# A transformer block on one core: the work ahead of the first projection in another order

## What is computed

```python
def _L0_attn_ref(x, Wqkv, bqkv, Wo, bo):           # 16 heads of 32
    kqv = x @ Wqkv + bqkv
    q, k, v = ...
    scores = einsum('bsnh,btnh->bnst', k, q) / sqrt(32)      # causal mask
    attn = softmax(scores, axis=2)
    return einsum('bnkq,bknh->bqnh', attn, v).reshape(b, s, 512) @ Wo + bo

def _L0_ffn_ref(h, gate_w, gate_scale, up_w, up_scale, down_w, down_scale):
    g, u = h @ Wg.T, h @ Wu.T                      # weights (int - 128) * scale
    return (silu(g) * u) @ Wd.T

x = x + _layernorm(_L0_attn_ref(_layernorm(x), ...))
x = x + _layernorm(_L0_ffn_ref(_layernorm(x), ...))
```

## Time and profile before

| | |
|---|---|
| median of 3 runs | 1654.09 us (1651.8 to 1659.24) |
| the profiled execution | 1659.15 us, its span 1657.3 us |
| PE busy over the span | 1552.0 us (94%) |
| DVE, ACT, POOL busy | 941.8, 775.8, 644.8 us |
| mean granted clock of PE | 0.975 |
| first transpose on PE | starts at 10.13 us |
| first projection on PE | starts at 30.95 us |
| first maximum (`mjob 0 0`) on PE | starts at 40.92 us |

### The profile page before, as it was taken

The page is one execution under the profiler, slowest core; times in us unless marked ns, Lnnn a source line. Parts: engine busy times, 40 slices in busy tenths (PEclk is TensorE's granted clock), DMA queues, the critical chain, the costliest instruction groups (busy, mean ns, idle before and its releaser), DMA issues.

```text
span 1657.3 us, 24457 instructions
## 1 busy us (share of the span) xinstructions
PE 1552.0 (94%) x9288; PEld 641.0 (39%) x9288; DVE 941.8 (57%) x1897; ACT 775.8 (47%) x1252; POOL 644.8 (39%) x844
## 2 busy tenths in 40 slices
PE   4899899988999899999897899999999999999997
PEld 2334234323333333343332244444444444444443
DVE  5657665778656777766777333464434343434344
ACT  5356566557566666755775643233222222222222
POOL 4336675677666677757766520020000000000001
PEclk8899999999999999999998999999999999999999
DMA  4222232213411233321354531221111111111000
GB/s 178 90 52 53 56 73 52 58 53 102 113 49 39 78 90 84 95 54 39 116 159 127 161 96 39 51 93 48 51 26 52 26 51 26 51 26 52 0 26 26
DMA packets 113397, 112.25 MB, mean 68 GB/s; under 512 B 69632, under 2 KB 69632, under 8 KB 113024
## 3 DMA queue, kind: packets, MB, share of 16 engines
q1 hardware_dynamic: 113280, 110.69, 23.5%
HBM read 45.37 MB, written 25.17 MB: 43 GB/s over the span
## 4 chain that ended last, share of the span: by engine, by line
PE 65%; POOL 13%; DVE 10%; ACT 6%; issue 5%; POOLq 0%; ACTq 0%; DVEq 0%
PE ps L966 25%; PE ps L887 13%; PE ps L983 12%; PE ps L950 9%; POOL pt L1452 5%; DVE mcol L1240 4%; PE ps L924 4%; ACT pt L1094 3%; POOL rs L1372 1%; PE ps L900 1%; POOL rec L1462 1%; POOL pt L1443 1%; POOL stage L1436 1%; DVE st L1135 1%; POOL atl L1466 1%
## 5 line engine op out<-in xcount | busy, mean ns | idle before, releaser
L1094 ACT ACTIVATE pt<-ps,nrm 128x512 f32<-128x512 f32 (+1 forms) x640 | 362.4, 645 | 264.6 <-PE ps L924 252.4
L966 PE MATMUL ps<-x2in,gu 128*128 128x512 f16 x2048 | 462.5, 379 | 0.1
L1240 DVE TENSOR_REDUCE mcol<-ps 128x1 f32<-128x512 f32 (+2 forms) x600 | 305.4, 575 | 134.3 <-PE ps L900 67.8
L966 PEld LDWEIGHTS ps<-x2in,gu 128*128 128x128 f16 x2048 | 200.2, 98 | 241.9 <-ACT sg L1115 0.5
L1369 POOL TENSOR_SCALAR rs<-mv 128x1 f32<-128x1 f32 x120 | 24.3, 202 | 655.6 <-DVE mv L1139 649.5
L1311 DVE SCALAR_TENSOR_TENSOR hf<-ps,usc,sg 128x512 f32<-128x512 f32 x128 | 96.1, 751 | 259.2 <-PE ps L966 246.5
L1120 ACT ACTIVATE hh<-hf 128x512 f16<-128x512 f32 x128 | 80.7, 631 | 258.9 <-DVE hf L1311 245.3
L1452 POOL TENSOR_TENSOR pt<-pt 128x1024 f32<-128x1024 f32 x84 | 201.4, 2419 | 0.0
L924 PE MATMUL ps<-qpack,kpack 98*128 98x512 f16 (+3 forms) x768 | 168.1, 335 | 32.5 <-DVE mcol L1240 23.6
L983 PE MATMUL ps<-wd,hh 128*128 128x512 f16 x496 | 188.0, 379 | 0.0
L983 PE MATMUL ps<-wd,hl 128*128 128x512 f16 x496 | 188.0, 379 | 0.0
(11 more groups left out here) (125 smaller groups left out, 1635.8 us busy)
## 6 DMA issues: line engine op xcount, KB each, us to landing
qpack<-stage SPq DMA_DIRECT2D x192, 64.0 KB, 2.0
kpack<-stage SPq DMA_DIRECT2D x192, 64.0 KB, 2.0
xr<-in_x SPq DMA_DIRECT2D x32, 256.0 KB, 2.9
x1d<-xr SPq DMA_DIRECT2D x32, 256.0 KB, 2.3
x2d<-xh SPq DMA_DIRECT2D x32, 256.0 KB, 2.0
x1in<-x1d SPq DMA_DIRECT2D x8, 1024.0 KB, 6.0
out_x<-yy SPq DMA_DIRECT2D x32, 256.0 KB, 2.0
xin<-in_x SPq DMA_DIRECT2D x24, 256.0 KB, 3.1
```

Source lines behind the costliest of these rows:

```text
L966: mm = pe.matmul(bk, GU[:, c, m, i * 128:(i + 1) * 128], x2in[:, 1 - k, p, c, :], start=p == 0 and c == 0, stop=p == 1 and c == 3)
L1094: act.activation(Pt[:, PBUF[step], h, off:512], ps[:, BANK[job], off:512], ACT.Exp, scale=esc).then_inc(s_ex, 1)
L1240: mm = dve.tensor_reduce(mcol[:, n % 2, col:col + 1], scores, AX.X, ALU.max)
```

## The change

The hand-written list is replaced. The first and last line of it, before and after, and the other edits:

```diff
-    plan += [("load_xs", 0), ("load_xs", 1), ("load_w", 0), ("load_xs", 2), ("load_xs", 3), ("load_bias",)]
...
-    plan += [("qk", 0, 1, 1), ("inverses", 2), ("split", 2), ("mjob", 0, 2), ("ones_rows", 0), ("packs", 0)]
+    plan += [("load_xs", 0), ("load_w", 0), ("load_xs", 1), ("load_w", 1), ("load_xs", 2), ("load_bias",), ("load_xs", 3)]
...
+    plan += [("norm_rest", 1), ("inverses", 1), ("qk_scale", 1), ("ln1_stats", 6), ("ln1_stats", 7), ("devs", 6)]
+    plan += [("ln1_turn", 4), ("ln1_turn", 5), ("ln1_norm", 6), ("ln1_norm", 7), ("qk", 0, 1, 0), ("ln1_turn", 6)]
...
+NORM_OPS = {}
+for job in PLAN:
+    if job[0] == "norm_max":
+        NORM_OPS.update({(job[1], i): len(NORM_OPS) + i for i in (1, 2)})
+    elif job[0] == "norm_rest":
+        NORM_OPS.update({(job[1], i): len(NORM_OPS) + i - 2 for i in (3, 4, 5, 6)})
...
-            return 6 * m + i
+            return NORM_OPS[m, i]
...
-                    if m == 3:
-                        continue
+                elif kind == "norm_rest":
+                    m = a[0]
                     sc_, lo_ = (2.0 / T ** 2, 2.0 ** -16) if m < 2 else (2.0 / 2.0 ** 26, 1e-30)
+                    e.wait_ge(s_cmax, NO["norm_max", m])
```

More of the change, by code:

```diff
@@ L193, in order_of_jobs @@
     add = plan.append
-    first = [[each for job in lot for each in with_dev(job)] for lot in staged(LN1, list(range(8)))]
-    plan += [("load_xs", 0), ("load_xs", 1), ("load_w", 0), ("load_xs", 2), ("load_xs", 3), ("load_bias",)]
[L197 to L205, removed]
@@ L206, in order_of_jobs @@
-    plan += [("inverses", 1), ("qk_scale", 1), ("split", 1), ("square", 2), ("qk", 0, 0, 0), ("qk", 0, 1, 0)]
-    plan += [("norms", 2), ("norm_max", 2), ("mjob", 0, 0), ("qk", 0, 0, 1), ("square", 3), ("mjob", 0, 1)]
-    plan += [("qk", 0, 1, 1), ("inverses", 2), ("split", 2), ("mjob", 0, 2), ("ones_rows", 0), ("packs", 0)]
+    plan += [("load_xs", 0), ("load_w", 0), ("load_xs", 1), ("load_w", 1), ("load_xs", 2), ("load_bias",), ("load_xs", 3)]
+    plan += [("load_w", 2), ("load_rows",), ("load_w", 3), ("ones_rows", 1)]
@@ new lines, in order_of_jobs @@
+    plan += [("ln1_stats", 0), ("ln1_stats", 1), ("devs", 0), ("ln1_norm", 0), ("ln1_norm", 1), ("square", 0)]
+    plan += [("ln1_turn", 0), ("ln1_turn", 1), ("norms", 0), ("ln1_stats", 2), ("ln1_stats", 3), ("devs", 2), ("norm_max", 0)]
+    plan += [("ln1_norm", 2), ("ln1_norm", 3), ("split", 0), ("square", 1), ("ln1_turn", 2), ("ln1_turn", 3), ("norms", 1)]
+    plan += [("ln1_stats", 4), ("ln1_stats", 5), ("devs", 4), ("norm_max", 1), ("bias_max",), ("norm_rest", 0)]
+    plan += [("inverses", 0), ("qk_scale", 0), ("split", 1), ("ln1_norm", 4), ("ln1_norm", 5), ("qk", 0, 0, 0)]
@@ new lines, in order_of_jobs @@
+    plan += [("norm_rest", 1), ("inverses", 1), ("qk_scale", 1), ("ln1_stats", 6), ("ln1_stats", 7), ("devs", 6)]
+    plan += [("ln1_turn", 4), ("ln1_turn", 5), ("ln1_norm", 6), ("ln1_norm", 7), ("qk", 0, 1, 0), ("ln1_turn", 6)]
+    plan += [("ln1_turn", 7), ("square", 2), ("norms", 2), ("norm_max", 2), ("norm_rest", 2), ("mjob", 0, 0), ("qk", 0, 0, 1)]
+    plan += [("square", 3), ("mjob", 0, 1), ("qk", 0, 1, 1), ("inverses", 2), ("split", 2), ("mjob", 0, 2)]
+    plan += [("ones_rows", 0), ("packs", 0)]
```

## The result

| | before | after |
|---|---|---|
| median, us | 1658.41 (11 runs, 1650.33 to 1659.32) | 1670.34 (11 runs, 1662.18 to 1671.20) |
| ratio to before, 95% interval | | 1.0075 (1.0056 to 1.0093) |
| profiled execution: time / span, us | 1659.15 / 1657.3 | 1662.95 / 1661.1 |
| PE busy in the first 100 us | 71.70 | 63.29 |
| first projection starts | 30.95 | 25.32 |

The change makes the kernel 0.75% slower. The direction was forecast, and the ratio of the forecast (1664.4 to 1654.09, 1.0062) lies in the measured interval. The time itself does not: 1670.34 is 5.94 us above the forecast and 0.84 above the end of its range. The ratio is estimated from all single times; it is not the quotient of the two medians, and the two can differ by about 0.1%. The profiled execution of the changed kernel, 1662.95, is the second shortest of its eleven.

A forecast was written before the change was run, and what follows sets the result against it. The first 100 us were taken as bound by a chain of waits through all engines, with `mjob 0 0` setting the time. 9.0 us there plus 1.3 of clock gave 10.3, on 1654.09: 1664.4 us, range 1657.5 to 1669.5.

The forecast's parts named there:

- The schedule: New lists followed job by job: first projection 5.5 us earlier, at 25.4, but `mjob 0 0` 9.0 us later, at 49.9.
- the early projection carries through: Rival, 3%: the projection at 25.4 sets the pace, `mjob 0 0` comes 5.5 us earlier, 1648.6 us.
- The clock behind `mjob 0 0`: Projection behind `mjob 0 0` runs on a slow clock after idle PE: 1.3 us more, middle of 0.7 to 2.0.
- The bound that the prediction named: Forecast wrong if `mjob 0 0` to the first score is more than 2 us shorter than before.
- the sum: Total loss: 9.0 us at `mjob 0 0` plus 1.3 of clock, 10.3 us.
- The clock comes up early: Rival, 15%: `norms 2` at 0.88 and the projection at 2.59, loss 8.0 us, 1662.1 us.
- POOL is crowded: Rival, 12%, with the clock staying down: `wl` beside `norm_rest 1` costs about 1 us more; 1666.1 to 1667 us.
- Part is absorbed: Rival, 12%: PE's waits before slow projections at 55.75 and 80.80 vanish, some 5 of 10.3 given back, 1659.4 us.
- the base: The sum was put on the median, 1654.09 us, as the profiled execution, 1659.15, was the slowest of those shown.
- nothing doubles: Behind `mjob 0 0` the chain moves with it: none of the loss is hidden and none doubles.
- The steps at nothing: The new order of loads, and the new wait on `s_cmax` in `norm_rest`, cost and gain nothing.

The follow-up runs named there:

- c_stats_early: Changed kernel with statistics and row scales of tiles 6 and 7 put ahead of weight 1's `norm_rest` and `inverses`: 1665.45 us, ratio 1.0053.
- d_front: Third order: the change's loads, split `norm_rest` and early first projection, but all statistics as soon as possible, weight 2 squared earlier: 1643.49 us, ratio 0.9934 to before.
- c_again: The changed kernel measured again without an edit: 1670.00 us, ratio 1.0086 to the kernel before.
- d_shift: Kernel before with three more fills (10.5 us in all) on POOL ahead of all row scales, same order: 1664.68 us, ratio 1.0054.
- e_after_warm: Changed kernel with eight matmuls whose result nobody reads ahead of the third `norms` on PE: 1665.46 us, ratio 1.0040 to before.
- e_after_small: Changed kernel with half a fill more (1.75 us) on POOL ahead of its work on the rows: 1670.94 us, ratio 1.0082 to before.
- e_front_split: `d_front` with `inverses 2` and `split 2` moved directly behind `mjob 0 0`: 1640.36 us, ratio 0.9898 to the kernel before.
- d_parts: Kernel before with only the change's load order and `norm_rest` split off, directly behind `norm_max` (weight 0: behind `bias_max`): 1655.92 us, ratio 1.0004.
- e_front_fill: `e_front_split` with POOL's fill of the packs moved behind the row scales of tiles 2 and 3: 1644.68 us, ratio 0.9922 to before.
- d_shift_small: Kernel before with half a fill more (1.75 us) on POOL ahead of the row scales: 1656.30 us, ratio 1.0010.
- c_square_early: Changed kernel with the third square moved behind the upper halves of tiles 2 and 3 on ACT: 1665.78 us, ratio 1.0058 to before.
- c_both_early: Changed kernel with the edits of both `c_square_early` and `c_stats_early`: 1661.67 us, ratio 1.0038 to before.

## Why the prediction was right, and where its size was wrong

**The schedule** came out as followed, job by job:

| step of the prediction | said | measured |
|---|---|---|
| first projection | 25.4 | 25.32 |
| its emptying on ACT | 33.4 | 33.35 |
| POOL: lower half, then the last four operations on weight 1 | 34.9, 36.1 to 37.6 | 34.84, 35.97 to 37.42 |
| DVE: statistics of tiles 6 and 7 | 38.0 | 37.86 |
| ACT: tiles 6 and 7 | 41.4 | 41.27 |
| third square | 45.2 | 44.97 |
| third `norms` on PE | 47.2 | 47.34 (three of its four matmuls are in the trace) |
| `mjob 0 0` | 49.9 | 49.70 |

The method is to take both lists, the prices of single operations from the trace, and the later of "own engine free" and "input there" at each step. The statement that ScalarE, VectorE and GpSimd queues are strict FIFO (the Trainium skill, TensorE: Matmul & The Clock Gate, Architectural detail) is borne out: DVE stood 3.25 us in front of a value of weight 1 with the rows of tiles 6 and 7 in memory. The rival "the early projection carries through" fell for that reason, and `c_stats_early` and `d_front` show that it falls by this order alone.

**The clock behind `mjob 0 0`** was put at 1.3 us. On the chain the projection takes 4.17 us against the 2.59 of before, 1.6 more, and 3.55 in `c_again`, 1.0 more. Up to the first score the term came out at 1.7 in one profile and at 0.1 in the other. The bound that the prediction named, from `mjob 0 0` to the first score, is 49.53 before, 51.20 after, 49.67 in `c_again` (where a later projection took 4.28 for the 5.11 of the earlier trace rows) and 48.32 with the clock up in `d_shift`. At the first score the changed kernel is 10.45 us later than before in one profile and 8.93 in the other; the sum said 10.3. "The clock comes up early" did not occur in either profile, though by the first score `c_again` was where that rival would have put it, give or take 1 us; `e_after_warm`, which forces it, measured 1665.46 with a ratio of 1.0040. "POOL is crowded" did not occur: its last operation on weight 1 took the quiet 0.57. "Part is absorbed" fell too: PE's stop that it would have had vanish is still there (2.41 us at 64.26), and nothing was given back in the medians.

**What failed, first: the base.** The forecast stood on the median of three executions, 1654.09; eleven gave 1658.41. These 4.3 us are most of the miss of 5.94. The prediction's own sum on the profiled execution, 1659.15 + 10.3 = 1669.5, would have been right to 0.9 us; the step that failed is to leave that execution because it was the slowest of three, and to take the middle of three for the level of the kernel. That the other choice would have hit is partly luck: the kernel before has medians of 1656.41, 1656.06 and 1657.09 in the other sets, 2 to 3 us above the base that was taken and 2 to 3 below 1659.15. In its four sets, of 11, 11, 23 and 17 executions, those under 1655 were 4, 3, 11 and 3.

**Second: the size of the difference.** The medians differ by 11.9 us (13.6 in `c_again`'s set), not by 10.3; this is the other 1.6 of the miss. The step was "nothing doubles": that whatever is late at `mjob 0 0` is found again at the end, unchanged. It is so in order and in waits, but not in the clock. Three landmarks of DVE show it. Before:

```profile
639.38 0.72 DVE L1281 SCALAR_TENSOR_TENSOR yt<-ps,nrm,bo_b 128x512 f32<-128x512 f32 x1
...
807.78 0.75 DVE L1281 SCALAR_TENSOR_TENSOR yt<-ps,nrm,bo_b 128x512 f32<-128x512 f32 x1 [0.34 <-PE ps L887]
...
976.42 0.75 DVE L1311 SCALAR_TENSOR_TENSOR hf<-ps,usc,sg 128x512 f32<-128x512 f32 x1 [2.10 <-ACT sg L1115]
```

After:

```profile
646.74 0.72 DVE L1287 SCALAR_TENSOR_TENSOR yt<-ps,nrm,bo_b 128x512 f32<-128x512 f32 x1
...
815.14 0.75 DVE L1287 SCALAR_TENSOR_TENSOR yt<-ps,nrm,bo_b 128x512 f32<-128x512 f32 x1 [0.34 <-PE ps L893]
...
980.25 0.75 DVE L1317 SCALAR_TENSOR_TENSOR hf<-ps,usc,sg 128x512 f32<-128x512 f32 x1 [2.09 <-ACT sg L1121]
```

`c_again`:

```profile
648.29 0.72 DVE L1287 SCALAR_TENSOR_TENSOR yt<-ps,nrm,bo_b 128x512 f32<-128x512 f32 x1
...
816.71 0.75 DVE L1287 SCALAR_TENSOR_TENSOR yt<-ps,nrm,bo_b 128x512 f32<-128x512 f32 x1 [0.34 <-PE ps L893]
...
985.51 0.75 DVE L1317 SCALAR_TENSOR_TENSOR hf<-ps,usc,sg 128x512 f32<-128x512 f32 x1 [2.10 <-ACT sg L1121]
```

`c_again` is behind by 8.9, 8.9 and 9.1: rigid from the first score on. The first profile of the changed kernel is behind by 10.45 at the first score, then 7.4, 7.4 and 3.8, so that it wins back 3.1 us ahead of the first landmark and 3.5 in the last 170 us of attention. Behind the last landmark all three take 680.9 us to the end. The clock of those 170 us stands in the windows; the column behind POOL's is the granted clock. Before, after and `c_again`, in this order:

```profile
815.00:985.00 170.00, 151.77 (x1130) 55.38 (x1129) 100.16 (x199) 103.71 (x173) 95.42 (x124) 0.94 0.46 136
```

```profile
815.00:985.00 170.00, 151.71 (x1150) 55.18 (x1150) 104.75 (x212) 106.28 (x178) 102.23 (x132) 0.96 0.46 134
```

```profile
815.00:985.00 170.00, 151.17 (x1132) 53.97 (x1131) 103.73 (x211) 104.82 (x175) 98.19 (x124) 0.94 0.43 125
```

So the same instructions in the same order take 886 us from the first score to the feed-forward, or 879 us, by where the clock falls. Of the 14 profiles nine have a stretch of 885.7 to 887.7 us (before and `c_again`, the other three of their set, `d_shift`, `e_after_small`, `e_after_warm`, `e_front_split`), four one of 877.7 to 879.4 (after, `d_parts`, `d_front`, `e_front_fill`), and `d_shift_small` lies between at 882.05. The profiled execution of the changed kernel is one of its rare short ones: of 17 executions 2 were under 1663, the others at 1668.19 to 1671.20. Before, 21 of 62 were under 1655. With 17 executions, 2 may still be chance.

That bears on the size, but it cannot be the whole rest: the longest executions of the two kernels, 1658.41 to 1659.32 and 1670.29 to 1671.20 in the first set, differ by as much as the medians. The executions that make the changed kernel's median were never profiled. Ten of its 17 took 1670.14 us or more, with a mean granted clock of 0.970 to 0.972; its two profiles are of 1662.95 (0.976) and 1668.19 (0.975), and of the 51 executions of the kernel before that have a clock on record none is under 0.974. An estimate from the rows above fits them: the late first score of the first profile (100.90), the stretch of `c_again` (886.1) and the 680.9 to the end give a span of 1667.9, a time of 1669.8, which is 10.6 us above the 1659.15 of before. The nearest profile is that of `e_after_small` (1671.80, clock 0.973), which does have both: 51.4 us from `mjob 0 0` to the first score, and a stretch of 885.95. What is left of the 11.9 is then that the median of before lies 0.7 below its profile, and some 0.6 that no run explains.

The versions that move the late places or bring the clock up do not show such executions: `c_square_early`, `c_stats_early`, `d_shift` and `e_after_warm` have mean clocks of 0.975 to 0.981 throughout, and `c_both_early` one of 0.973 among five of 0.976 and 0.977. At the first score `d_shift` and `e_after_warm` are 7.8 and 7.1 us later than before, and their medians 8.6 and 8.4. So the lowest clocks go with this order at the start, `e_after_small` included (two of its six are at 0.970 and 0.971). Where in the execution that clock is lost, and why the start should decide it, is **not settled**: no profile shows it.

**The steps at nothing** held: loads and `norm_rest` showed no difference in 12 runs, with an interval of 0.9988 to 1.0021. The trace shows a gain of 0.4 us at the first projection of `d_parts` that the prediction didn't have, below what the medians can tell.

## What to carry over

When an order by hand is changed, follow the new list on every engine to the first job behind which nothing has changed, and read the gain there, not at the job that was pulled forward. Ask at each wait what stands behind it in the same in-order queue: here four scalar operations of POOL held the statistics of two tiles, and through them PE. And take more executions than three as the base when the difference that you forecast is no larger than their spread.
